# Subtracting the softmax maximum on VectorE instead of TensorE for half of the score banks, with a new order of all instruction streams

## The reference

```python
x = x + jnp.tanh(g_xattn[0]) * _L0_xattn_ref(ctx_1024, ctx_1024, _layernorm(x, axis=-1), ...)   # stage A
x = x + jnp.tanh(g_ffn[0]) * _L0_ffn_ref(_layernorm(x, axis=-1), ...)                            # stage B
x = x + jnp.tanh(g_xattn[1]) * _L1_xattn_ref(_layernorm(x, axis=-1), ctx_1024, ...)              # stage C
x = x + jnp.tanh(g_ffn[1]) * _L1_ffn_ref(_layernorm(x, axis=-1), ...)                            # stage D
```

```python
score = jnp.einsum('bhij,bhkj->bhik', k, q) / jnp.sqrt(jnp.asarray(dh, k.dtype))
attn = jax.nn.softmax(score, axis=1)
out = jnp.einsum('bhik,bhij->bhjk', attn, v)
```

## Time and profile before

| | |
|---|---|
| time, median of 3 runs | 2642.75 us (2641.51 to 2643.96) |
| profiled execution | 2644.14 us, span 2642.3 us |
| TensorE busy | 2542.6 us, 96% |
| TensorE weight loads | 2212.0 us, 84% |
| VectorE busy | 2158.8 us, 82% |
| ScalarE busy | 1637.7 us, 62% |
| GpSimd busy | 1472.6 us, 56% |
| mean granted TensorE clock | 0.997 of full speed |

### The profile page before, as it was taken

The page is one execution under the profiler, slowest core; times in us unless marked ns, Lnnn a source line. Parts: engine busy times, 40 slices in busy tenths (PEclk is TensorE's granted clock), DMA queues, the critical chain, the costliest instruction groups (busy, mean ns, idle before and its releaser), DMA issues.

```text
span 2642.3 us, 70830 instructions
## 1 busy us (share of the span) xinstructions
PE 2542.6 (96%) x28238; PEld 2212.0 (84%) x28238; DVE 2158.8 (82%) x4124; ACT 1637.7 (62%) x3210; POOL 1472.6 (56%) x1808
## 2 busy tenths in 40 slices
PE   6999999999999999999999999999999999999998
PEld 4888888888888888888888888888888888888886
DVE  6788888888888888888888888888888888888874
ACT  4466666666666666666666666666666666666663
POOL 4455655655556556556556556556556556556552
PEclk9999999999999999999999999999999999999999
DMA  2000101001001001001001001001011011010000
GB/s 99 12 21 29 32 16 32 28 20 32 28 20 32 28 20 32 28 20 32 28 20 32 28 20 32 23 25 32 17 32 32 16 32 32 16 32 28 20 29 13
DMA packets 74316, 73.12 MB, mean 28 GB/s; under 512 B 6555, under 2 KB 73393, under 8 KB 74290
## 3 DMA queue, kind: packets, MB, share of 16 engines
q1 hardware_dynamic: 74290, 72.75, 8.9%
HBM read 54.90 MB, written 16.78 MB: 27 GB/s over the span
## 4 chain that ended last, share of the span: by engine, by line
PE 35%; ACT 19%; DVE 16%; issue 12%; SPq 8%; DMA 7%; POOL 3%; POOLq 0%; DVEq 0%; ACTq 0%
PE work L1628 8%; DMA x_ln<-xp 7%; PE work L1629 6%; PE work L1630 6%; SPq L288 4%; PE work L1667 4%; ACT e L684 4%; PE scores L1710 3%; DVE h_f L1149 3%; DVE act_g L1146 3%; PE scores L1721 3%; ACT xn_C L641 3%; DVE work L1164 2%; PE work L1651 2%; SPq L279 2%
## 5 line engine op out<-in xcount | busy, mean ns | idle before, releaser
L684 ACT ACTIVATE e<-scores 120x1024 f32<-120x1024 f32 x512 | 502.5, 1022 | 43.2 <-PE scores L1731 32.2
L1628 PE MATMUL work<-xt_hi_B,w_hi 128*128 128x256 f32 x1536 | 446.5, 291 | 0.8 <-DVE h_f L1149 0.3
L1629 PE MATMUL work<-xt_lo_B,w_hi 128*128 128x256 f32 x1536 | 433.7, 282 | 0.0
L1630 PE MATMUL work<-xt_hi_B,w_lo 128*128 128x256 f32 x1536 | 433.0, 282 | 0.0
L383 POOL TENSOR_TENSOR h_lo<-h_f,h_hi 128x256 fp32r<-128x256 f32 x384 | 279.4, 735 | 238.6 <-ACT h_hi L634 236.8
L389 POOL TENSOR_TENSOR zt<-e 120x512 f32<-120x512 f32 x256 | 322.4, 1280 | 106.9 <-ACT e L684 106.9
L1628 PEld LDWEIGHTS work<-xt_hi_B,w_hi 128*128 128x128 f32 x1536 | 290.2, 189 | 24.3 <-DVE xt_lo_B L1135 1.6
L1155 DVE TENSOR_REDUCE m<-scores 120x128 fp32r<-120x2048 f32 x128 | 292.0, 2281 | 4.1 <-PE scores L1721 4.0
L1629 PEld LDWEIGHTS work<-xt_lo_B,w_hi 128*128 128x128 f32 x1536 | 289.4, 188 | 5.7
L1168 DVE TENSOR_TENSOR e<-e,work 120x2048 f32<-120x2048 f32 x128 | 292.0, 2281 | 2.2
L634 ACT ACTIVATE h_hi<-h_f 128x256 fp32r<-128x256 f32 x384 | 159.4, 416 | 210.5 <-DVE h_f L1149 210.5
(11 more groups left out here) (209 smaller groups left out, 7196.7 us busy)
## 6 DMA issues: line engine op xcount, KB each, us to landing
x_ln<-xp SPq DMA_DIRECT2D x64, 256.0 KB, 2.9
x_res<-xp SPq DMA_DIRECT2D x64, 256.0 KB, 2.7
y<-y_out SPq DMA_DIRECT2D x64, 256.0 KB, 2.2
ctx_f_A<-cp SPq DMA_DIRECT2D x64, 128.0 KB, 2.6
ctx_f_C<-cp SPq DMA_DIRECT2D x64, 128.0 KB, 2.5
qm<-mT SPq DMA_DIRECT2D x256, 4.0 KB
e<-wi SPq DMA_DIRECT2D x3, 768.0 KB, 5.3
w_ctx<-wc SPq DMA_DIRECT2D x1, 656.0 KB
```

The costliest lines, as they stand in the source:

```text
L684: return act.activation(e[0:SC, c, 2 * h:2 * h + 2, :, :].rearrange("p a b n -> p (a b n)"), scores[0:SC, 2 * h:2 * h + 2, :].rearrange("p ...
L1628: pe.matmul(out, a_hi, b_hi_, start=first, stop=False, skip_group_check=parts)
L1629: pe.matmul(out, a_hi, b_lo_, start=False, stop=False, skip_group_check=parts)
L1630: last = pe.matmul(out, a_lo, b_hi_, start=False, stop=end, skip_group_check=parts)
```

## The change

VectorE gets a function `subtract_max(c, h)` that subtracts m0 from two score banks in place, and does so for h = 1, the upper two banks, for both chunks. TensorE keeps h = 0. ScalarE's exponential of the upper banks waits for VectorE's semaphores (`A0_sub_dve`, `A1_sub_dve`).

`DEPTH` goes from 4 to 5, and the order of every queue is new: in prologue, loop and epilogue. The loop runs 59 turns. Turn t now works on batch t in stage A's layer norm, t-1 in its scores, t-2 in stage B, t-3 in C's first part, t-5 in D. The work of a batch is the same apart from the subtraction. `keep_busy` matmuls are 160 instead of 170.

```diff
-DEPTH = 4
+DEPTH = 5
...
+            def subtract_max(c, h):
+                banks = scores[0:SC, 2 * h:2 * h + 2, :].rearrange("p r (h n) -> p (r h) n", n=P)
+                row = m0[0:SC, c:c + 1, :].bitcast(F32).to_broadcast([SC, 8, P])
+                return dve.tensor_tensor(banks, banks, row, ALU.subtract)
...
-                act.wait_ge(s["A0_sub"], nth(1, 2, t))
-                exponential(e0, 0, 1).then_inc(s["A0_exp"], 1)
...
+                act.wait_ge(s["A0_sub_dve"], t)
+                exponential(e0, 0, 1).then_inc(s["A0_exp"], 1)
...
-                subtract_max(1, 1).then_inc(s["A1_sub"], 1)
...
-                subtract_max(0, 0).then_inc(s["A0_sub"], 1)
-                subtract_max(0, 1).then_inc(s["A0_sub"], 1)
...
+                subtract_max(0, 0).then_inc(s["A0_sub"], 1)
```

More of the change, by code:

```diff
@@ new lines, in _ @@
+            dve.wait_ge(s["A1_z"], 4)
+            reciprocal0(W[1], 1).then_inc(s["A1_rz"], 1)
+            dve.wait_ge(s["A1_rz"], 4)
+            normalise(W[1], 1).then_inc(s["A1_p"], 1)
+            dve.wait_ge(s["T_hi_A"], 4)
+            transposed_lo("A", W[0]).then_inc(s["T_lo_A"], 1)
+            dve.wait_ge(s["A1_mm"], 4)
+            head_max(1).then_inc(s["A1_max"], 1)
+            dve.wait_ge(s["yA_hi"], 4)
+            low(y_lo["A"][:, :, :], two(W[2], KC), y_hi["A"][:, :, :]).then_inc(s["yA_lo"], 1)
@@ new lines, in _ @@
+            dve.wait_ge(s["A1_mm"], 5)
+            head_max(1).then_inc(s["A1_max"], 1)
+            dve.wait_ge(s["A1_max"], 5)
+            subtract_max(1, 1).then_inc(s["A1_sub_dve"], 1)
+            dve.wait_ge(s["yA_hi"], 5)
+            low(y_lo["A"][:, :, :], two(W[2], KC), y_hi["A"][:, :, :]).then_inc(s["yA_lo"], 1)
+            gated(0, W[1]).then_inc(s["G_a"], 1)
+            dve.wait_ge(s["G_a"], 24)
+            hidden(0, W[1]).then_inc(s["G_h"], 1)
+            dve.wait_ge(s["G_h"], 24)
@@ new lines, in _ @@
+            hidden(4, W[1]).then_inc(s["G_h"], 1)
+            dve.wait_ge(s["G_h"], 28)
+            reciprocal0(W[1], 1).then_inc(s["A1_rz"], 1)
+            dve.wait_ge(s["G_tanh"], 28)
+            gated(5, W[2]).then_inc(s["G_a"], 1)
+            dve.wait_ge(s["G_a"], 29)
+            dve.wait_ge(s["G_lo"], 28)
+            hidden(5, W[2]).then_inc(s["G_h"], 1)
+            normalise(W[1], 1).then_inc(s["A1_p"], 1)
+            dve.wait_ge(s["dn_mm"], 30)
+            residual(x2, x1, W[0]).then_inc(s["res_B"], 1)
@@ new lines, in _ @@
+            dve.wait_ge(s["res_B"], 5)
+            moments("C", x2, FIRST).then_inc(s["ln_eps_C"], 1)
+            dve.wait_ge(s["woA_mm"], 5)
+            residual(x1, x_res, W[3]).then_inc(s["res_A"], 1)
+            dve.wait_ge(s["res_A"], 5)
+            moments("B", x1, FIRST + 1).then_inc(s["ln_eps_B"], 1)
+            dve.wait_ge(s["T_hi_C"], 6)
+            transposed_lo("C", W[3]).then_inc(s["T_lo_C"], 1)
+            dve.wait_ge(s["ld_x_ln"], 96)
+            moments("A", x_ln, FIRST + 4).then_inc(s["ln_eps_A"], 1)
@@ new lines, in _ @@
+            key_scores(0).then_inc(s["M0_mm"], 1)
+            down(W[1], 1).then_inc(s["dn_mm"], 1)
+            pe.wait_ge(s["res_C"], LAST + 1)
+            gate_up(W[2], 5).then_inc(s["G_mm"], 1)
+            pe.wait_ge(s["M0_max"], LAST + 1)
+            scores0(1).then_inc(s["A1_mm"], 1)
+            maxima_transposed(W[0]).then_inc(s["mT_mm"], 1)
+            down(W[1], 2).then_inc(s["dn_mm"], 1)
+            pe.wait_ge(s["mT_out"], LAST + 1)
+            pe.wait_ge(s["yA_lo"], LAST + 1)
```

2409 lines of the change are left out of this document (1314 added, 1095 removed), and 9 rows, old and new, of tables (given, passing).

## The result

The changed kernel takes 2565.95 us in the median of four runs (2557.85 to 2581.56), the kernel before 2642.32 beside it: a ratio of 0.9717 (95% interval 0.9668 to 0.9767). Run again later against its own neighbours it took 2557.94 (five runs, 2556.73 to 2560.68), ratio 0.9663 (0.9649 to 0.9677). The profiled execution of the first measurement took 2557.85. The forecast was 2538, range 2500 to 2595. The first median lies 28 us above it, the repeated one 20.

The account below looks back on a forecast made before the run. TensorE's queue was taken to bound the kernel, with VectorE nearly full after the change. A walked turn of 37.9 plus 0.35 gave 38.25; 59 x 38.25 + 280.8 = 2537.6, forecast 2538 us, range 2500 to 2595.

Parts of the forecast that it names:

- TensorE's relief: On TensorE, two subtraction pairs fewer (0.94 us) and fewer switches of matmul kind (0.19): 1.13 us less a turn.
- VectorE's subtraction: On VectorE, two new 120x1024 subtractions in PSUM at 1.22 us each, 2.44 a turn; busy time becomes 35.66.
- Late turns go: At VectorE's moments of x_ln, the load issued earlier no longer comes late: 0.38 us less a turn.
- The walk: One turn of the new order followed from C's transposes to hidden(1), VectorE nearly full: 37.9 us.
- the margin: Over the whole turn, 0.35 us added to 37.9 for turns that now and then lose something: 38.25 taken.
- three waits of TensorE: In a turn, TensorE waits 0.3 us before keys_values1, 0.5 for xt_lo_D at f1, 0.2 before scores0(1).
- rival 3: TensorE never waits because VectorE's pieces are dense: turn toward 37.4 us, 2488 us in all; chance 0.06.
- The ends: Outside the loop's 59 turns, filling, draining and five passes' work take 280.8 us.
- slower rival: VectorE keeps its 6.7 us of waits a turn: turn of 42.4, 2783 us in all; chance 0.05.
- "waits unchanged" end: Upper end for the turn: all waits stay as they are and only TensorE's 1.13 us goes, 38.8 us.
- Rival 2: At the turn's end, TensorE waits for late maxima or hidden(1): turn 38.8 to 39.8, at 39.2 2594 us; chance 0.17.
- the signs: In the profile after, TensorE's waits headed by xt_lo_D or the key maxima, and by hidden(1) at the turn's start.

Follow-up runs that it names:

- e1: Changed kernel (new order, lag of five) with all subtractions given back to TensorE: 2599.08 us, 0.9819 of the kernel before.
- e11: Changed kernel with hidden_lo(3) behind weigh, chunk 0's subtraction on TensorE and chunk 0's key maps early on ScalarE: 2527.75 us, 0.9556 of the kernel before.
- e2: Kernel before, in its old order, with only the upper banks' subtraction moved to VectorE: 2655.33 us, 1.0031 of the kernel before.
- e5: Changed kernel with GpSimd's hidden_lo(3) made to wait until VectorE's weigh is done: 2538.58 us, 0.9602 of the kernel before.
- e3: Kernel before with one edit, the x_ln load issued ahead of the maxima's DMAs: 2616.81 us, 0.9887 of the kernel before.
- e4: Changed kernel run again without edits, for its spread: 2557.94 us, 0.9663 of the kernel before.
- e6: Changed kernel with chunk 0's subtraction given back to TensorE, VectorE keeping chunk 1's: 2542.68 us, 0.9614 of the kernel before.
- e9: e1 with GpSimd's addition to x_res moved from ahead of hidden_lo(3) to behind y_lo_C: 2568.45 us, 0.9710 of the kernel before.

## Why the prediction was right, and what was wrong in it

**TensorE's relief (-1.13 a turn): right in size.** Its busy time fell by 81.0 us, 1.27 for each of 64 batches. The pairs are 0.92 of it: in e1 a turn without its 0.8 of waiting is 38.44, in e11, with one pair fewer, 37.98. That this relief shortens the turn whatever the order was tacitly assumed, and wrong: e2 makes the same relief in the old order and is slower by 0.3%.

**VectorE's subtraction (1.22 each): right**, 1221 ns measured; busy in a turn 35.78 for 35.66 (35.42 in e5, where `weigh` is not held).

**Late turns go (-0.38): right**, shown by e3 alone, with 0.45.

**The walk (37.9) and the margin (38.25): the step that failed.** The walk went to VectorE by one branch alone: TensorE to `keys_values1`, ScalarE's copies of the keys, and from their end VectorE without rest to `hidden(1)`. Counted like the walk from the first transposes of C (medians over the turns):

| | walk | changed | e5 |
|---|---|---|---|
| `keys_values1` starts | 8.8 | 8.97 | 8.97 |
| ScalarE's last copy ends | 11.3 | 11.44 | 11.44 |
| VectorE's reciprocal starts | 11.3 | 11.94 | 11.48 |
| `hidden(1)` ends | 37.9 | 38.37 | 38.01 |
| turn | 37.9 | 38.49 | 38.11 |

The branch itself was right within 0.15, and so was the 26.5 us of VectorE behind it (26.4 in the changed kernel). (The pieces add up to 37.8, not 37.9.) What it lacked is the other branch into the same reciprocal, `attended1`, the transposes yz_q, `weigh` and y1f. With `weigh` at 0.76 as before the two end together; held by `hidden_lo` it takes 1.30, and the reciprocal waits for y1f. Of the 0.59 between 37.9 and 38.49, 0.38 went with that hold in e5; the other 0.21 are the walk's small shortfalls.

The prediction's own numbers could have shown it. Its three waits of TensorE, 0.3, 0.5 and 0.2, add up to 1.0, and rival 3 puts a turn without waits at 37.4: together 38.4, for which 37.9 leaves no room. Measured from start to start are 0.27 at `keys_values1`, 0.71 at `f1`, none at `scores0(1)`, and 37.51 without waits: 38.49.

That 38.25 came within 0.24 is luck in part. The 0.35 added to the walk was the amount by which before's mean turn lies above its quick one (0.38 by its own rows), and that unevenness was the x_ln load (e3), already counted as gained. It happened to cover over half of what the walk lacked. Of the 18.5 us by which the profiled span exceeds the 2537.6 worked out, 59 x 0.24 = 14.2 are this term.

**The ends (280.8): 285.2**, 4.4 of the 18.5. The first median is another 8 above its profiled execution, by the spread that e4 did not show again.

**The rivals.** The rule of the Trainium skill that was weighed ("Perfetto Trace Analysis", section "Identifying the Most-Contended Engine") judges TensorE by its FLOPs or by the busy share of its weight loads, and VectorE by its busy share; its reason is that pipelined matmuls look smaller in a trace, not that they flatter. By it VectorE (90% of the span after) stands above the weight loads (84%), which was the prediction's argument for its slower rival. It wasn't slower, but the chain after gives VectorE 47%, and e6, which takes 1.22 us off it, gains 0.5% against the changed kernel though TensorE gets 0.47 back. So VectorE is no longer beside the path, as the prediction's "waits unchanged" end had it; it is half of it. Rival 2's mechanism, a store and maxima that come late at the turn's end, did not come: `scores1(1)` follows the transposes without a wait. Rival 3's bound, TensorE without a wait, is 37.98 - 0.47 = 37.51 by e11, for the 37.4 given. Of the signs, xt_lo_D does head TensorE's waits; the key maxima and `hidden(1)` are not among them.

**What the order gives back.** In parts of the ratio: the early load 1.1%, the rest of the order 0.7%, the move 1.6%, together the 3.4% of the repeated run. The parts hold for this path only, since each new arrangement has another clash. The middle term hides one of 0.55 us a turn, which the move happens to undo. With e9 in place of e1, the rest of the order is worth 1.8% and the move 0.5%; with `weigh` cured too (e5) the move is worth 1.1%.

## What to carry to other kernels

When a change reorders queues, look for what will run beside what, not only what waits for what: durations from the old trace hold only for the old neighbours, above all for VectorE and GpSimd. When two engines are both over 85% busy, find the closed cycle that sets the turn and ask of each edit whether it lies on it, and then check in the new trace what it has moved beside what: the same work moved for the other chunk made 58 us here, and much of that by a clash that no one had planned. And try the smallest part of a change alone: one load issued earlier was a third of this one's gain, and the headline edit by itself no gain.

## What the runs showed of the hardware

A VectorE instruction can be held until an instruction of GpSimd ends, and the other way round, whole instructions at a time. A 128x2 TENSOR_SCALAR between SBUF tiles took 1.33 us instead of 0.17 beside GpSimd's addition of 1.29 that started 0.01 later and ended 0.03 earlier (by the profile's starts), and 0.17 again when that was moved (e9). A lead of 0.01 to 0.02 us in these starts doesn't say who is held: in e5 var_eps_A started 0.02 ahead of the addition in nearly all turns, took 0.16 in most and 1.33 in two. A product of two SBUF tiles, 128x256, took 0.96 instead of 0.43 (1307.01 to 1307.97, the second of the pair above), and GpSimd's of the same size 1.01 instead of 0.73. Two operations with an operand in PSUM were not held. The subtraction, which reads and writes PSUM, took from 1215 to 1233 ns in its 128 instances, chunk 1's with GpSimd at work beside it (from 1332.09 for 0.46). `normalise`, which reads one operand from PSUM, took 2.28 at 1337.10 with two of GpSimd's operations beside it, and 2.28 in the mean before.

The Trainium skill, "SBUF — State Buffer", section "SBUF: two separate sides", says that VectorE and GpSimd share one pair of ports, that whichever starts first has it for the whole instruction, and that it concerns VectorE's operations with two SBUF inputs or in its two-port mode. The traces of e1, e5 and e9 agree that a hold lasts for the whole instruction, with the numbers above. In which mode neg_mean_A ran, which has one SBUF input, and who started first where the starts lie 0.01 apart, no run here shows. The rule was not weighed in the prediction, which has no term for GpSimd beside VectorE.
